# Four graph layers on one Trainium2 core: A's two halves split on PE and ACT, the last mixed rows stored in their own tile

## What is computed

```python
support = x @ W0;  h = segment_sum(support[src] * edge_weight, dst) + b0        # layer 0
w = einsum('rb,bio->rio', att, basis)                                          # layer 1, twice (relu between)
agg = segment_sum(where(type == 0, gate0 * x_j @ w[0], gate1 * x_j @ w[1]), row) + x @ root + bias
out = segment_sum(deg^-1/2[src] * deg^-1/2[tar] * (x @ W2.T + b2)[tar], src) + ...   # layer 2
p = exp(q[rows] . k[cols] / 8 + att_bias - row_max); out = (p v / sum p) @ Wo + bo   # layer 3
```

## Time and profile before

| | us |
|---|---|
| median of 3 runs (lowest, highest) | 1412.52 (1408.61, 1424.08) |
| profiled execution, its own time | 1410.63 |
| span of that execution | 1408.8 |
| mean granted TensorE clock | 0.953 of full |
| busy: PE, DVE, ACT, POOL | 1216.7, 882.0, 432.3, 376.3 |

### The profile page before, as it was taken

One profiled execution on the slowest core, in us unless ns is written; L12 is line 12 of the kernel. 1 busy time (PEld: TensorE's weight loads), 2 busy tenths in 40 slices (PEclk: granted clock), 3 DMA queues, 4 the chain that ended last, 5 costly groups with the idle time before them and its releaser, 6 DMA issues.

```text
span 1408.8 us, 21905 instructions
## 1 busy us (share of the span) xinstructions
PE 1216.7 (86%) x8327; PEld 562.4 (40%) x8328; DVE 882.0 (63%) x1189; ACT 432.3 (31%) x574; POOL 376.3 (27%) x220
## 2 busy tenths in 40 slices
PE   6767677599597999999999999787777699999996
PEld 2233333133242333344445534443333355555552
DVE  7559678244244555543588736447776588878886
ACT  2357567122132121113110021343340243433431
POOL 1010210000100344445556645545557100000000
PEclk9989988799799999999999999999999799999998
DMA  8688883995498788751222121122221565556452
GB/s 322 235 273 262 291 269 77 369 342 198 148 353 277 269 259 255 216 178 3 32 39 39 17 62 3 2 22 21 21 22 32 179 212 182 181 178 208 146 182 73
DMA packets 108301, 227.05 MB, mean 161 GB/s; under 512 B 74728, under 2 KB 79592, under 8 KB 91990
## 3 DMA queue, kind: packets, MB, share of 16 engines
q1 hardware_dynamic: 34872, 157.71, 32.8%
q0 software_dynamic: 68704, 53.43, 15.4%
q10 hardware_dynamic: 4638, 14.69, 2.9%
HBM read 201.56 MB, written 62.55 MB: 187 GB/s over the span
## 4 chain that ended last, share of the span: by engine, by line
DMA 36%; PE 26%; issue 13%; POOL 12%; DVE 8%; ACT 2%; DVEq 2%; SPq 1%; ACTq 1%; POOLq 0%; PEldq 0%
DMA bias_d<-R 25%; POOL bias_d L717 12%; PE PS L1659 5%; PE PS L1897 4%; PE PS L1884 4%; DMA W<-R 3%; PE PS L1914 3%; DVE R L1118 2%; PE PS L1530 2%; PE PS L1512 2%; DMA key_d<-R 2%; PE PS L1903 2%; PE PS L1568 2%; DMA R<-R 1%; PE PS L1634 1%
## 5 line engine op out<-in xcount | busy, mean ns | idle before, releaser
L717 POOL DMA_INDIRECT bias_d<-R x160 | 334.2, 2089 | 365.7 <-DMA bias_d<-R 217.5
L1659 PE MATMUL PS<-R 128*128 128x512 f16 x1300 | 297.8, 382 | 18.2 <-DVE R L881 16.7
L1659 PEld LDWEIGHTS PS<-R 128*128 128x128 f16 x1300 | 121.5, 98 | 200.4 <-issue 66.5
L1476 ACT ACTIVATE R<-PS 128x1024 f32<-128x1024 f32 (+1 forms) x100 | 100.5, 1005 | 172.3 <-PE PS L1884 172.2
L1634 PE MATMUL PS<-W,XX 128*128 128x512 f16 x600 | 136.6, 387 | 16.4 <-DMA W<-w_d 15.0
L1083 DVE CUSTOM_DVE_ANT_0 R<-PS,R 128x1250 f16<-128x1250 f32 x80 | 116.8, 1460 | 47.8 <-PE PS L1823 46.3
L1118 DVE SCALAR_TENSOR_TENSOR R<-R,W 128x1024 f32<-128x1024 f32 (+1 forms) x68 | 133.6, 1990 | 17.4 <-ACT R L1476 11.9
L1568 PE MATMUL PS<-R,XX 125*128 125x512 f16 (+1 forms) x480 | 102.6, 358 | 48.3 <-DVE R L826 41.5
L687 POOL DMA_DIRECT2D bias_d<-bias_d x39 | 27.2, 705 | 344.8 <-DMA W<-w_d 182.9
L1884 PE MATMUL PS<-R 128*128 128x256 f16 (+3 forms) x800 | 106.7, 276 | 8.7 <-DMA R<-max_d 8.2
L1897 PE MATMUL PS<-R 128*32 128x256 f32 (+1 forms) x1600 | 105.7, 382 | 5.1 <-DVE R L1118 4.5
(11 more groups left out here) (217 smaller groups left out, 1441.6 us busy)
## 6 DMA issues: line engine op xcount, KB each, us to landing
bias_d<-bias_d POOLq DMA_DIRECT2D x39, 1280.0 KB, 13.6
R<-in_basis_s SPq DMA_DIRECT2D x48, 1024.0 KB, 6.6
W<-bias_d SPq DMA_DIRECT2D x27, 1024.0 KB, 5.0
R<-bias_d SPq DMA_DIRECT2D x13, 1024.0 KB, 4.8
W<-in_basis_s SPq DMA_DIRECT2D x12, 1024.0 KB, 6.7
R<-key_d SPq DMA_DIRECT2D x20, 500.0 KB, 4.1
R<-R SPq DMA_DIRECT2D x80, 80.0 KB, 7.6
W<-bias_d SPq DMA_DIRECT2D x7, 904.0 KB, 4.6
```

The costliest lines, as they stand in the source:

```text
L717: pool.indirect_dma_start(bias_d, bass.IndirectOffsetOnAxis(ap=idx[0:EC, c:c + 1], axis=0), attr[0:EC, c, :], None, bounds_check=DUMP + GC ...
L1476: S.activation(ER[:, n % 4, :].rearrange("p (h r) -> p h r", h=4)[:, :, 0:w], PS[:, 2 * (n % 2):2 * (n % 2) + 2, :].rearrange("p a (e r) - ...
L1659: ins = T.matmul(mm_out(4 + i % 2, D), lhs, rhs, start=n == 0, stop=n == len(terms) - 1)
```

## The change

1. **Split of A.** ACT copies all 128 rows of a tile as fp16 into stage16. SP stores rows 96 to 127 of it as A16[:, 0]: the high part of the sum of high weights. A constant fix16 has the identity in rows 64 to 95 and minus the identity in rows 96 to 127, in the columns 96 to 127, and zeros elsewhere. PE adds fix16 times stage16 to the same banks (function fix, three matmuls), so that rows 96 to 127 hold high sum + low sum - stored copy, and ACT copies that to A16[:, 1]. The fix of tile j - 1 stands in tile j, ahead of its last three visits. The additions and subtractions of DVE, the copy a0_high of ACT and the buffers ah and al are gone.
2. **1250 columns.** One-hot matrices and build matmuls cover REAL (1250 columns) instead of PIECES (1280). DVE clears the 30 columns left in two banks once.
3. **Buffers.** key and the two `more` matrices move from W to R3. The basis buffers in W come first in BASIS_1, so SP loads two bases at tile 32 of the build. The next two and x follow when all is stored and the last fix is done (before: two bases and x when all is stored, two more when a0_made is complete).
4. **Waits.** SP no longer waits for a0_made between groups. PE starts the product of layer 0 when all stores have landed (before: a0_made). DVE waits for x only ahead of the first norm, no longer ahead of the first mixes.
5. **mix_stored.** ACT issues the last store to w_d in the tile (i = 7) in which the last mixes are made, no longer behind tile 9.

```diff
-        ah = [in_w(NN) for b in range(2)]
-        al = [in_w(NN // 2).bitcast(F16) for b in range(2)]
-        key = in_w(CH)
+        o = 8 * D
...
+        fix16 = in_w(P // 2).bitcast(F16)
+        zero = r3[:, NT * D + 2 * NN + CH:NT * D + 3 * NN + CH]
         more = zero.bitcast(F16).rearrange("p (s r) -> p s r", s=MORE)
-        minus16 = in_w(P // 2).bitcast(F16)
+        key = r3[:, NT * D + 2 * NN:NT * D + 2 * NN + CH]
...
-        BASIS_1 = [four(r3, NT * D), four(r3, NT * D + 4 * D), four(w_b, 0), four(w_b, 4 * D)]
+        BASIS_1 = [four(w_b, 0), four(w_b, 4 * D), four(r3, NT * D), four(r3, NT * D + 4 * D)]
...
# SP
-                if j == 0 and k >= 2:
-                    sp.wait_ge(a0_made, k - 1)
...
-                sp.wait_ge(evicted, t + 3)
+                if t == 32:
+                    for m in range(M0, M0 + 2):
+                        load_basis(m)
+                sp.wait_ge(copied, t + 1)
+                sp.dma_start(A16[32 * j:32 * j + 32, 0, k, :], stage16[96:128, j, :]).then_inc(stored[j], 16)
...
-                sp.dma_start(al[k % 2][32 * j:32 * j + 32, :], stage16[64:96, j, 0:NN]).then_inc(stored[j], 16)
...
-            for m in range(M0, M0 + 2):
+            sp.wait_ge(fixed_up, TT)
+            for m in range(M0 + 2, M0 + 4):
                 load_basis(m)
             sp.dma_start(X.rearrange("p k f -> p (k f)"), a["x"]).then_inc(x_in, 16)
-            sp.wait_ge(a0_made, NT)
-            for m in range(M0 + 2, M0 + 4):
-                load_basis(m)
...
# DVE
+            V.memset(fix16[:, 0:96], 0.0)
+            V.tensor_tensor(fix16[:, 96:128], ident16[:, 64:96], ident16[:, 96:128], ALU.subtract).then_inc(fix_made, 1)
...
-            def windows(t4, lag, b):
-                rngs = tile_ranges(dve, t4)
-                make(rngs[0], t4, 0)
-                if lag > 1:
-                    a0_low(t4 - 2, b)
-                make(rngs[1], t4, 1)
-                make(rngs[2], t4, 2)
-                make(rngs[3], t4, 3)
-                if lag > 0:
-                    asum(t4 - 1, 1 - b)
+            def windows(t4):
+                rngs = tile_ranges(dve, t4)
+                for j in range(4):
+                    make(rngs[j], t4, j)
...
# ACT
-                    S.activation(stage16[0:96, j, 0:NN], banks[0:96, 0:NN], ACT.Copy)
-                    S.activation(ah[0 if b is None else 1 - b][32 * j:32 * j + 32, :], banks[96:128, 0:NN],
+                    S.activation(stage16[:, j, :], banks[:, 0:NN], ACT.Copy).then_inc(copied, 1)
+                    act.wait_ge(fixed_up, t4 * 4 + (j + 1))
+                    S.activation(flat(A16[32 * j:32 * j + 32, 1, bass.ds(t4, 1), :]), banks[96:128, 0:NN],
                                  ACT.Copy).then_inc(evicted, 1)
...
+                if MIXES - 1 in mixes_of(i):
+                    mix_stored(MIXES // 2 - 1)
                 deviation(0, i)
-            mix_stored(MIXES // 2 - 1)
...
# PE
+            def fix(t4, j):
+
+                pe.wait_ge(copied, t4 * 4 + (j + 1))
+                for b, (p0, p1) in enumerate(REAL):
+                    ins = T.matmul(mm_out(3 * (j % 2) + b, p1 - p0), fix16[:, :], stage16[:, j, p0:p1], start=False,
+                                   stop=True, skip_group_check=True)
+                ins.then_inc(fixed_up, 1)
...
-                    for b, (p0, p1) in enumerate(PIECES):
+                    for b, (p0, p1) in enumerate(REAL):
...
+                if j:
+                    fix(t4, j - 1)
+                elif not first:
+                    fix(t4 - 1, 3)
                 for m in range(1, FIXED):
                     ins = fixed(m)
...
-            pe.wait_ge(a0_made, NT)
+            for j in range(4):
+                pe.wait_ge(stored[j], 48 * (NT + 1))
```

More of the change, by code:

```diff
@@ L825, in fixed @@
                 def fixed(m):
-                    V.tensor_scalar(hot[0:EC, FIXED * (j % 2) + m, :], iota16[0:EC, :], base[0:EC, bass.ds(t4, 1), j],
+                    V.tensor_scalar(hot[0:EC, FIXED * (j % 2) + m, 0:NODES], iota16[0:EC, 0:NODES], base[0:EC, bass.ds(t4, 1), j],
                                     key[0:EC, bass.ds(lo + m, 1)], ALU.add, ALU.is_equal).then_inc(hot_made, 1)
@@ L833, in make @@
                     dve.wait_ge(more_used, v + 1)
-                    V.tensor_scalar(flat(more[0:EC, bass.ds(v & (MORE - 1), 1), :]), iota16[0:EC, :],
+                    V.tensor_scalar(flat(more[0:EC, bass.ds(v & (MORE - 1), 1), 0:NODES]), iota16[0:EC, 0:NODES],
                                     base[0:EC, bass.ds(t4, 1), j], key[0:EC, bass.ds(c, 1)], ALU.add,
@@ L869, in _ @@
             V.scalar_tensor_tensor(b16[:, :, :], b16[:, :, :], lowrow, brow, ALU.mult, ALU.add).then_inc(b16_made, 1)
-            with dve.Fori(1, 2) as t4:
-                windows(t4, 1, 1)
-            with dve.Fori(1, NT // 2) as t:
-                for e in range(2):
-                    windows(t * 2 + e, 2, e)
-            dve.wait_ge(a0h_made, NT - 1)
-            V.tensor_tensor(A16[:, 1, NT - 2, :], ah[0], A16[:, 0, NT - 2, :], ALU.subtract).then_inc(a0_made, 1)
-            for j in range(4):
-                dve.wait_ge(stored[j], 48 * (NT + 1))
-            V.tensor_tensor(ah[1], ah[1], al[1], ALU.add).then_inc(asum_made, 1)
-            dve.wait_ge(a0h_made, NT)
-            V.tensor_tensor(A16[:, 1, NT - 1, :], ah[1], A16[:, 0, NT - 1, :], ALU.subtract).then_inc(a0_made, 1)
+            with dve.Fori(1, NT) as t4:
+                windows(t4)
             def turned_low(n, i):
@@ L1250, in _ @@
             act.wait_ge(tab_in, 16)
-            def a0_high(k, b):
-                act.wait_ge(asum_made, k + 1)
-                S.activation(flat(A16[:, 0, bass.ds(k, 1), :]), ah[b], ACT.Copy).then_inc(a0h_made, 1)
-            def group(t4, b=None, again=True):
+            act.wait_ge(pad_zero, 1)
+            with act.Fori(0, NT) as t4:
                 for j in range(4):
@@ L1261, in group @@
                     act.wait_ge(stored[j], t4 * 48 + 48)
-                    if j == 0 and again:
-                        act.wait_ge(a0_made, t4 - 1)
                     banks = PS[:, 3 * (j % 2):3 * (j % 2) + 3, :].rearrange("p a b -> p (a b)")
-                    S.activation(stage16[0:96, j, 0:NN], banks[0:96, 0:NN], ACT.Copy)
-                    S.activation(ah[0 if b is None else 1 - b][32 * j:32 * j + 32, :], banks[96:128, 0:NN],
+                    S.activation(stage16[:, j, :], banks[:, 0:NN], ACT.Copy).then_inc(copied, 1)
+                    act.wait_ge(fixed_up, t4 * 4 + (j + 1))
+                    S.activation(flat(A16[32 * j:32 * j + 32, 1, bass.ds(t4, 1), :]), banks[96:128, 0:NN],
                                  ACT.Copy).then_inc(evicted, 1)
-                    if j == 2 and b is not None:
-                        a0_high(t4 - 1, b)
-            group(0, None, False)
-            group(1, 0, False)
-            with act.Fori(1, NT // 2) as t:
-                for e in range(2):
-                    group(t * 2 + e, 1 - e)
             act.wait_ge(sup_out, 32)
@@ L1278, in _ @@
                 act.dma_start(SUP[:, q, :, :], sup_d[:, q, :, :]).then_inc(sup_in[q], 16)
-            act.wait_ge(asum_made, NT)
-            S.activation(A16[:, 0, NT - 1, :], ah[1], ACT.Copy).then_inc(a0h_made, 1)
             def transposed(n, i):
@@ L1560, in _, with build @@
             pe.wait_ge(tab_in, 16)
-            def build(rng, j, t4):
+            def fix(t4, j):
[4 more added lines that the diff above has]
+                ins.then_inc(fixed_up, 1)
+            def build(rng, j, t4, first):
                 lo, hi, off = rng
                 def visit(c, hots, first):
-                    for b, (p0, p1) in enumerate(PIECES):
+                    for b, (p0, p1) in enumerate(REAL):
                         ins = T.matmul(mm_out(3 * (j % 2) + b, p1 - p0),
@@ L1588, in _ @@
             pe.wait_ge(own_made, 1)
-            with pe.Fori(0, NT) as t4:
-                rngs = tile_ranges(pe, t4)
-                for j in range(4):
-                    build(rngs[j], j, t4)
-            pe.sem_inc(a_built, 1)
+            pe.wait_ge(fix_made, 1)
+            for lo, hi in ((0, 1), (1, NT)):
+                with pe.Fori(lo, hi) as t4:
+                    rngs = tile_ranges(pe, t4)
+                    for j in range(4):
+                        build(rngs[j], j, t4, lo == 0)
+            fix(NT - 1, 3)
             def turn(n, i):
```

28 lines of the change are left out of this document (12 added, 16 removed).

## The result

The changed kernel takes 1424.22 us (median of 20 runs, 1413.55 to 1427.62), the kernel before on the same chip 1414.18 (20 runs): ratio 1.0063 [1.0039, 1.0087]. The ratio and its interval are formed from the fast executions of both, so it is not quite the quotient of the two medians. The forecast was 1416, within 1% of the kernel before. The time came out 0.6% longer: within 1%, as said, but with an interval that leaves out 1: a small loss. The profiled execution has a span of 1422.6 us (before: 1408.8).

What follows compares the result with a forecast made beforehand. Bound by a chain through 160 successive scatters, so only the first scatter's start counts: -8 - 3 - 3.2 + 19 = +4.8 us on 1410.6 gives 1415.4, said as 1416; own range 1400 to 1428, range with rivals 1380 to 1436.

Steps and rivals of the forecast that it cites:

- The build, -8: Building CT and A16 over 40 tiles: shorter groups -14 us, stores under fill bursts +6, net -8 us.
- PE's tile is then 6.1 x 0.527 + 0.42 = 3.63 us: Build on PE: 6.1 visits of 0.527 us plus 0.42 for gaps make a tile of 3.63 us.
- the hand-over closes just in time: Build, between PE and ACT: second copy ends at about 3.45 us, PE wants that bank at 3.6.
- A tile of 4 us or more with PE idle ahead of the fix matmuls: Sign of being wrong, in the build: the hand-over between PE and ACT is too tight.
- The stops for stores: In the build: DVE's 26.5 us of waits go; fill bursts still cost 6 us, from 0 to 29.
- The second rival: Fills of bias_d hold the build's stores, ACT waits 29 us instead of 6: 1438 us; chance 0.15.
- To the first product, -3: Between build and first product: PE starts 13.7 us after the build instead of 16.7, -3 us.
- The basis wait, -3.2: First product: two basis loads are made at tile 32, so PE's wait at 271.93 goes, -3.2 us.
- What that lets loose, +19: Behind the product's end T: fills delay edge loads, DVE and PE stall, first scatter at T + 119.1, +19 us.
- The first rival: Behind T, the edge loads come through the fills in time and 16 us stay gained: 1380 us; chance 0.21.
- The rest: From the first scatter on: 160 scatters one after another, nothing touched, everything behind them follows.

Runs made afterwards that it cites:

- e1: The kernel before with only the last store to w_d moved into tile 7 of the product; 1429.16 us, ratio 1.0122 to the kernel before.
- e2: The changed kernel with the last store to w_d put back behind tile 9; 1400.77 us, ratio 0.9932 to the kernel before.
- e3: The changed kernel with POOL waiting for the five loads of edge lists and attr ahead of its last 13 fills; 1392.42 us, ratio 0.9866 to the kernel before.

## Why the prediction was right, and where its terms were off

Its sum was -8 - 3 - 3.2 + 19 = +4.8 us. Measured on the profiled pair, first scatter to first scatter, it is +10.1, and 13.8 over the span; the rest arose in the scatter stage and behind it.

- *The build, -8: the term that failed.* From PE's start the build gained 1.8 us, and this execution began 2.1 us later: +0.3 in all. The step that failed is "PE's tile is then 6.1 x 0.527 + 0.42 = 3.63 us" with "the hand-over closes just in time". Of visits it was right; the gaps were taken from the idle column (0.22), which counts from a modelled end. A visit is issued in 0.53 us but shown as 0.70, so a gap from issue to issue is 0.17 longer, 0.38. And of the hand-overs only those from PE to ACT had a time, 0.2 us each; those from ACT back to PE had none, where the rows show 0.35 from the first copy to the fix and 0.46 from the second copy to the next tile. 6 x 0.527 + 2 x 0.38 = 3.92 is the tile as measured. Forty tiles 0.29 us longer are 12 us; the stores gave back 5 of the 6 counted for them, and so the build ended 6 us above the 167 forecast. A tile of 4 us or more with PE idle ahead of the fix matmuls was named as a sign of being wrong, and it is nearly that.
- *The stops for stores.* They went as said: 39 us of waits of DVE and ACT became 0.6. The second rival, fills that hold the build's stores (+23), didn't come: I took 6 us and it was 0.6.
- *To the first product, -3:* -5.1; the loads of SUP landed in 7.4 us at the median instead of 8.8, and PE began 11.6 us behind the build instead of 13.7. *The basis wait, -3.2:* as said, T - product start fell from 104.8 to 101.7.
- *What that lets loose, +19:* +17.9. Attr was to complete at T + 58.5, and DVE ran again at T + 60.1; the last product was to be read at T + 96.3, and ACT read it at T + 97.0 (454.49); first scatter T + 119.1, measured 118.0. e1 shows this term in the kernel before, e2 its absence in the changed one, and e3 that it hangs on the order of fills and loads alone. The first rival (1380) didn't come; e3 gets by a wait the 16 us that it had behind T, but stays at 1392, since the build gave next to nothing.
- *The rest.* 3.7 us of the 13.8 lie behind the first scatter, which the prediction held to follow unchanged. The median of one and the same kernel moves by such sizes from one set of executions to another (1402.75 to 1414.18 for the kernel before in five sets), and no run here ties them to the change.

The time came out within 1% because gains half as large as forecast (7.8 us up to T, not 14.2) met one loss of the size forecast. The loss and its cause were foreseen. That the wrong tile did not spoil the forecast is luck: the miss of 6 us up to T happens to be smaller than the range of 1%.

## What to carry to other kernels

Before making a transfer's release earlier, look at what else is released at that moment: a queue with large packets that starts together with one of small rows can make the small one many times slower (5.2 against 57.2 us here), and an explicit wait that lets the small one go first held the large ones back by 8 us and took 2% off the changed kernel's time (from 1.0063 to 0.9866 of the kernel before). When work is passed back and forth between two engines once a tile, write down every circle with its hand-overs (0.2 to 0.5 us each here) and not the busy time alone, and don't move a step to help one circle without adding up the other.
